# Target one-hots of the edge counts: from one VectorE comparison to two ScalarE activations

## The chip, the cores and the metric

One core of a Trainium2 chip runs the kernel as one program. The time is the device time of one execution in microseconds (us); the median of several runs is given. The core's engines are TensorE (PE in the profile, with its weight loads as PEld), VectorE (DVE), ScalarE (ACT), GpSimd (POOL) and SyncE (SP), which issues most transfers.

## What is computed (the reference)

A graph of N = 1250 nodes with 768 features and 20000 edges (sorted by target) passes two graph networks, each followed by a residual sum and a layer norm:

```python
loops = jnp.arange(N)
src = jnp.concatenate([edge_index[0], loops])
dst = jnp.concatenate([edge_index[1], loops])
x1 = jax.nn.relu(x @ W_ah + b_ah)
# three attention layers on x1, their outputs joined and projected
e = jax.nn.leaky_relu(as_n[src] + ad_n[dst], 0.2)
p = jnp.exp(e - jax.ops.segment_max(e, dst)[dst])
out = segment_sum(p / segment_sum(p, dst)[dst] * h[src], dst)
```

The kernel never walks over edges in the attention layers. It turns the edge list once into a dense table of counts, how many edges lead from node s to node d with the node's own loop added, and multiplies by it. The first stage makes this table, and x1 beside it.

## The kernel before

The first stage is `counts_and_x1`. It works in ten tiles of T = 125 target nodes. The edges stand in 40 columns of 4 x 125; since they are sorted by target, the edges of one tile lie in a few neighbouring columns. DVE works out for every tile the first column, the number of columns and the number of columns before it (lines 216 to 241, into `range_i`). A column is a run of RUN = 4 groups of 125 edges, one edge to a partition.

For a tile, `count(t)` on TensorE first writes the own loops into `p_count` (line 382, three matmuls of a shifted band), and then for every group of 125 edges multiplies two one-hot matrices (line 388): `dst_hot`, 125 edges by 125 target nodes of the tile, is the stationary side, and `src_hot`, 125 edges by 1250 source nodes, the moving side, in three pieces of 418, 416 and 416 columns. Their product adds each edge to the cell of its pair. DVE makes both one-hots by comparing the row of node numbers `node_no` with the edge's own number, a column of `edge_col` (lines 254 and 255), in `one_hots(t)`. Four buffers of each stand in a ring: `hot_ready` tells TensorE that a pair is there, `hot_free` tells DVE that a buffer is read. The number of runs is known only on the chip, so `one_hots` and `count` are loops over a register, and each begins by loading two or three registers from `range_i` (lines 246 to 248 on DVE, 378 and 379 on TensorE).

Around this, in an order written out by hand for each engine, stands other work, five times for a pair of tiles b:

- TensorE: count the even tile, turn a piece of x (line 417), make a part of x1 (line 431, three matmuls for each product of split operands), turn the counted row (line 401), count the odd tile, the rest of x1, turn the next x, turn the odd row, turn x again.
- DVE: one-hots of the even tile, the low parts of x (line 269), score weights (line 502), the mask (line 260), the low part of x1 (line 276), one-hots of the odd tile, then score weights, mask and low parts again.
- ACT: `round_x` (line 322, the rounded part of x), `stage_row` (line 309, the counts from PSUM to SBUF), `keep_x1` (lines 335 and 339), `keep_turned` (line 316, the turned row into the table `CT`). It does nothing while TensorE counts.

ACT's order in the loop is:

```python
round_x(b, 2)
stage_row(b * 2)
keep_x1(b, 0)
keep_turned(b * 2)
stage_row(b * 2 + 1)
keep_x1(b, 1)
keep_x1(b, 2)
round_x(b + 1, 0)
keep_turned(b * 2 + 1)
round_x(b + 1, 1)
```

POOL makes the constants and splits the weights of x1, and SP loads x. At the end of the stage all engines meet at a barrier, after which `project` begins at its line 575 (loads) and line 717 (TensorE).

Of the kernel before, what the change touches and what calls it, by code (L numbers as in the profile page):

```python
# [4 lines left out]
F32 = mybir.dt.float32  # L5
F32R = mybir.dt.float32r
BF16 = mybir.dt.bfloat16
# [3 lines left out]
ALU = mybir.AluOpType  # L11
ACT = mybir.ActivationFunctionType
# [5 lines left out]
T = 125  # L18
NT = N // T
KD = D // 128  # L20
RUN = 4
ER = E // (RUN * T)
# [79 lines left out]
def counts_and_x1(nc, core, src, dst, x, w_ah, b_ah, w_gat, a_gat):  # L102
# [4 lines left out]
    with ExitStack() as ctx:  # L107
        sb, pb, sem = core.tools(ctx)
        dst_ends = sb("dst_ends", [ER, 2], F32)
        ends_row = sb("ends_row", [128, 2, ER], F32)  # L110
        edge_col = sb("edge_col", [T, 2, RUN, 2 * ER], F32)
# [7 lines left out]
        range_i = sb("range_i", [1, 3, NT], I32)  # L119
        node_no = sb("node_no", [T, N], I16)  # L120
        src_hot = sb("src_hot", [T, RUN, N], BF16)
        dst_hot = sb("dst_hot", [T, RUN, T], BF16)
        band = sb("band", [T, 2 * N - T], BF16)
        ident_b = sb("ident_b", [T, T], BF16)
        zeros_b = sb("zeros_b", [T, T], BF16)
# [7 lines left out]
        bias = sb("bias_ah", [128, KD], F32)  # L133
# [16 lines left out]
        cols_ready = sem("cols_ready")  # L150
        ranges_ready = sem("ranges_ready")
        hot_ready = sem("hot_ready")
        hot_free = sem("hot_free")
        counted = sem("counted")
        row_staged = sem("row_staged")
        mask_done = sem("mask_done")
# [32 lines left out]
        @block.gpsimd  # L189
        def _(pool):  # L190
            pool.iota(node_no[:], [[1, N]], base=0, channel_multiplier=0).then_inc(consts, 1)
            pool.iota(tile_lo, [[T, NT], [0, ER]], base=0, channel_multiplier=0).then_inc(consts, 1)
            pool.iota(run_no, [[0, NT], [1, ER]], base=0, channel_multiplier=0).then_inc(consts, 1)
            for m in (band, ident_b, zeros_b):
                pool.memset(m[:], 0.0).then_inc(consts, 1)
            pool.wait_ge(consts, 6)
            pool.affine_select(out=ident_b[:], in_=ident_b[:], compare_op=ALU.not_equal, fill=1.0, base=0,
                               pattern=[[-1, T]], channel_multiplier=1).then_inc(consts, 1)

            pool.affine_select(out=band[:], in_=band[:], compare_op=ALU.not_equal, fill=1.0, base=N - T,  # L200
                               pattern=[[-1, 2 * N - T]], channel_multiplier=1).then_inc(consts, 1)
            for k in range(KD):
                pool.wait_ge(w_in[k % 2], 16 * (k // 2 + 1))
                pool.tensor_copy(w_hi[:, k, :], w_raw[:, k % 2, :]).then_inc(w_split, 1)
                pool.wait_ge(w_split, 2 * k + 1)
                pool.tensor_tensor(w_lo[:, k, :], w_raw[:, k % 2, :], w_hi[:, k, :].bitcast(F32),
                                   ALU.subtract).then_inc(w_split, 1)
            weighed.loads(pool, lambda n: w_gat[n // KD, n % KD * 128:(n % KD + 1) * 128, :].rearrange("p (u c) -> p u c", u=1),
                          lambda g: a_gat[g:g + 1].rearrange("o a c -> o (a c)").broadcast_to([128, 2 * PAIR]))

        @block.vector
        def _(dve):
# [32 lines left out]
            def one_hots(t):  # L245
                first = dve.value_load(range_i[0:1, 0, bass.ds(t, 1)], min_val=0, max_val=ER - 1)
                count = dve.value_load(range_i[0:1, 1, bass.ds(t, 1)], min_val=1, max_val=ER)
                before = dve.value_load(range_i[0:1, 2, bass.ds(t, 1)], min_val=0, max_val=ER * NT)
                with dve.Fori(0, count) as j:
                    for h in range(RUN):  # L250

                        dve.wait_ge(hot_free, (before + j) * RUN + (h + 1))
                        at = bass.ds(first + j, 1)
                        v.tensor_scalar(src_hot[:, h, :], node_no[:], edge_col[:, 0, h, at], None, ALU.is_equal)
                        v.tensor_scalar(dst_hot[:, h, :], node_no[:, bass.ds(t * T, T)], edge_col[:, 1, h, at],  # L255
                                        None, ALU.is_equal).then_inc(hot_ready, 1)

            def mask(t):
                dve.wait_ge(row_staged, t + 1)
# [36 lines left out]
        @block.scalar  # L296
        def _(act):

            nc.scalar.sem_inc(mask_done, 1)

            act.wait_ge(bias_in, 16)

            def stage_row(t):

                act.wait_ge(counted, t + 1)
                act.wait_ge(mask_done, t + 1)
                act.wait_ge(row_turned, t * 3 + 1)
                for i, (a, w) in enumerate(CH):
                    last = nc.scalar.activation(count_row[:, a:a + w], p_count[:, i, 0:w], ACT.Copy)
                last.then_inc(row_staged, 1)  # L310

            def keep_turned(t):
                for i in range(3):
                    k = 4 if i < 2 else 2
                    act.wait_ge(row_turned, t * 3 + (i + 2))
                    nc.scalar.activation(CT[:, 4 * i:4 * i + k, bass.ds(t * T, T)],
                                         p_turn[0:T, i, 0:k * T].rearrange("p (k q) -> p k q", q=T),
                                         ACT.Copy).then_inc(ct_done, 1)

            def round_x(b, g):  # L320
                act.wait_ge(x_turned, b * 3 + (g + 1))
                nc.scalar.activation(xT_hi[:, 2 * g:2 * g + 2, :],
                                     p_x[:, g % 2, 0:2 * BT].rearrange("p (k n) -> p k n", k=2),
                                     ACT.Copy).then_inc(xhi_done, 1)

            def keep_x1(b, g):
                act.wait_ge(x1_summed, b * 3 + (g + 1))
                if g == 0 and b:
                    act.wait_ge(x1_lo_done, b * 3)
                if g == 2:  # L330
                    act.wait_ge(x1_lo_done, b * 3 + 1)
                if g == 1 and b:
                    act.wait_ge(x1_lo_done, b * 3 - 1)
                for m in range(2):
                    last = nc.scalar.activation(x1_f[:, g % 2, m * BT:(m + 1) * BT], p_x[:, (g + 1) % 2, m * BT:(m + 1) * BT],
                                                ACT.Relu, bias=bias[:, 2 * g + m:2 * g + m + 1])
                last.then_inc(x1_relu, 1)
                act.wait_ge(x1_relu, b * 3 + (g + 1))
                nc.scalar.activation(x1T[0][:, 2 * g:2 * g + 2, bass.ds(b * BT, BT)],
                                     x1_f[:, g % 2, :].rearrange("p (k n) -> p k n", k=2),  # L340
                                     ACT.Copy).then_inc(x1_hi_done, 1)

            round_x(0, 0)
            round_x(0, 1)
            for b in range(NB):
                round_x(b, 2)
                stage_row(b * 2)
                keep_x1(b, 0)
                keep_turned(b * 2)
                stage_row(b * 2 + 1)  # L350
                keep_x1(b, 1)
                keep_x1(b, 2)
                if b + 1 < NB:
                    round_x(b + 1, 0)
                keep_turned(b * 2 + 1)
                if b + 1 < NB:
                    round_x(b + 1, 1)

        @block.tensor
        def _(pe):  # L360
# [16 lines left out]
            def count(t):  # L377
                count_ = pe.value_load(range_i[0:1, 1, bass.ds(t, 1)], min_val=1, max_val=ER)
                before = pe.value_load(range_i[0:1, 2, bass.ds(t, 1)], min_val=0, max_val=ER * NT)

                for i, (a, w) in enumerate(CH):
                    nc.tensor.matmul(p_count[:, i, 0:w], ident_b[:], band[:, bass.ds(t * -T + (N - T + a), w)],
                                     start=True, stop=False, skip_group_check=True)
                with pe.Fori(0, count_) as j:
                    for h in range(RUN):
                        pe.wait_ge(hot_ready, (before + j) * RUN + (h + 1))
                        for i, (a, w) in enumerate(CH):
                            last = nc.tensor.matmul(p_count[:, i, 0:w], dst_hot[:, h, :], src_hot[:, h, a:a + w],  # L388
                                                    start=False, stop=False, skip_group_check=True)
                        last.then_inc(hot_free, 1)  # L390
                nc.tensor.matmul(p_count[:, 0, 0:2], zeros_b[:], src_hot[:, 0, 0:2], start=False, stop=True,
                                 skip_group_check=True).then_inc(counted, 1)
# [1633 lines left out]
```

## Time and profile before

| | us |
|---|---|
| median of 3 runs | 2172.72 (2171.94 to 2173.78) |
| the profiled execution, its own time | 2165.81 |
| its span, first to last instruction | 2164.0 |
| mean granted TensorE clock | 0.941 of full speed |
| PE busy | 1872.8 (87%) |
| PEld busy | 1785.0 (82%) |
| DVE busy | 1483.7 (69%) |
| ACT busy | 963.4 (45%) |
| POOL busy | 199.6 (9%) |

All times in the profile count from the span's start. The counting with its x1 work takes the stretch from 26 us to 262 us. An instruction group has a count, a busy time, a mean duration, and the idle time that its engine had just before such instructions, with what ended it ("issue" is time in which the engine waited for nothing that the profile shows). An engine's instructions overlap a little: the next starts before the last has ended, so that a pitch (start to start) is shorter than a duration. A line with a small q behind the engine (DVEq) is the engine's sequencer: registers, branches, waits.

### The profile page before, as it was taken

What the parts mean: (1) busy time and instruction counts of PE and PEld (TensorE: products, weight loads), DVE (VectorE), ACT (ScalarE), POOL (GpSimd) and SP (SyncE); (2) the same over time, 40 slices, a digit from 0 to 9 for tenths busy, and PEclk for the clock granted to TensorE, in tenths of its full rate; (3) what the DMA queues carried; (4) which work ended last, traced back from release to release, by engine and by line L of the source; (5) the groups of instructions that cost most, each with busy time, mean ns of one, the idle gap of its engine ahead of it and who ended that gap; (6) DMA issues with size and microseconds to landing.
All of it is one profiled execution on the core that took longest, in us unless ns stands there. A gap on an engine that the chain in (4) does not pass through costs nothing. (4 is left out here: it accounts for less than half of the span.)

```text
span 2164.0 us, 30233 instructions
## 1 busy us (share of the span) xinstructions
PE 1872.8 (87%) x11452; PEld 1785.0 (82%) x11452; DVE 1483.7 (69%) x2447; ACT 963.4 (45%) x1446; POOL 199.6 (9%) x161
## 2 busy tenths in 40 slices
PE   5999899967999999952999799969999968995993
PEld 4666699967999999952999599969999968995993
DVE  7887689978888889721565449348888863335842
ACT  1222221217779787830232322257888853333411
POOL 5010021200000000000000101100000000004500
PEclk9999999988999999976999899989999989998997
DMA  3121145344234333146655456473243217455002
GB/s 112 47 70 48 63 129 152 98 114 123 80 87 114 105 108 86 60 135 173 191 152 162 128 151 173 134 181 99 84 139 96 75 56 222 108 136 131 1 1 72
DMA packets 203526, 237.73 MB, mean 110 GB/s; under 512 B 99598, under 2 KB 178534, under 8 KB 203394
## 3 DMA queue, kind: packets, MB, share of 16 engines
q1 hardware_dynamic: 193314, 204.09, 33.5%
q0 software_dynamic: 9312, 29.14, 4.7%
q10 hardware_dynamic: 768, 2.70, 0.4%
q8 instruction: 87, 1.43, 0.3%
q14 instruction: 45, 0.37, 0.1%
HBM read 173.99 MB, written 61.90 MB: 109 GB/s over the span
## 5 line engine op out<-in xcount | busy, mean ns | idle before, releaser
L946 PE MATMUL p_o<-h_in,p 125*125 125x193 f32 x2400 | 405.7, 332 | 42.6 <-ACT res L843 21.7
L946 PEld LDWEIGHTS p_o<-h_in,p 125*125 125x125 f32 x2400 | 399.5, 191 | 45.9 <-issue 24.7
L1669 PE MATMUL p_y<-fw_hi,f_hi 128*125 128x384 f32 (+1 forms) x680 | 236.1, 347 | 88.3 <-DVE f_lo L1543 87.5
L866 ACT ACTIVATE e<-uv,col 125x1250 f32<-125x1250 f32 x240 | 298.5, 1359 | 17.3 <-DMA uv<-uv_rows 15.0
L1404 PE MATMUL p_o<-p_hi,h_parts 125*128 125x416 f32 (+1 forms) x960 | 282.6, 355 | 25.2 <-DVE p_lo L1338 19.0
L1669 PE MATMUL p_y<-fw_lo,f_hi 128*125 128x384 f32 (+1 forms) x680 | 233.7, 344 | 0.0
L1669 PE MATMUL p_y<-fw_hi,f_lo 128*125 128x384 f32 (+1 forms) x680 | 233.2, 343 | 0.0
L900 DVE TENSOR_TENSOR e<-e 125x1250 f32<-125x1250 f32 x120 | 174.1, 1451 | 67.6 <-ACT e L866 67.5
L1543 DVE TENSOR_TENSOR f_lo<-f_raw,f_hi 128x1125 fp32r<-128x1125 f32 (+1 forms) x80 | 101.1, 1265 | 169.4 <-ACT f_hi L1643 169.4
L1643 ACT ACTIVATE f_hi<-f_raw 128x1125 fp32r<-128x1125 f32 (+1 forms) x80 | 87.4, 1093 | 275.0 <-PE p_y L1669 221.0
L1404 PEld LDWEIGHTS p_o<-p_hi,h_parts 125*128 125x128 f32 x960 | 181.6, 189 | 31.2 <-issue 19.2
L1669 PEld LDWEIGHTS p_y<-fw_hi,f_hi 128*125 128x125 f32 x680 | 129.7, 191 | 91.4 <-issue 90.0
L646 DVE CUSTOM_DVE_ANT_0 max_junk<-src_row,G 125x1250 bf16<-125x1250 f32 x120 | 185.8, 1615 | 4.3 <-DMA src_row<-score_rows 3.7
L733 PE MATMUL p_h<-pw_hi,x1T 128*125 128x384 f32 x720 | 186.3, 340 | 0.0
L905 DVE SCALAR_TENSOR_TENSOR p<-e,CT 125x1250 f32<-125x1250 f32 x120 | 175.3, 1461 | 6.9 <-PE p_o L946 3.0
L1146 PE MATMUL p_h<-pw_hi,x2T 128*125 128x256 f32 x960 | 172.6, 283 | 0.0
L1404 PE MATMUL p_o<-p_lo,h_parts 125*128 125x416 f32 (+1 forms) x480 | 169.9, 354 | 0.0
L1146 PEld LDWEIGHTS p_h<-pw_hi,x2T 128*125 128x125 f32 x960 | 147.6, 188 | 0.0
L388 PE MATMUL p_count<-src_hot,dst_hot 125*125 125x416 bf16 (+1 forms) x588 | 126.3, 371 | 17.6 <-DVE dst_hot L255 17.6
L1296 ACT ACTIVATE e<-uv,col 125x416 f32<-125x416 f32 (+1 forms) x240 | 139.6, 629 | 0.0
L1146 PE MATMUL p_h<-pw_lo,x2T 128*125 128x256 f32 x480 | 135.8, 283 | 0.0
L388 PEld LDWEIGHTS p_count<-src_hot,dst_hot 125*125 125x125 bf16 x588 | 73.8, 145 | 70.4 <-DVE dst_hot L255 53.8
(220 smaller groups left out, 3330.7 us busy)
## 6 DMA issues: line engine op xcount, KB each, us to landing
f_raw<-turned SPq DMA_DIRECT2D x40, 562.5 KB
f_raw<-turned SPq DMA_DIRECT2D x40, 500.0 KB
h_rows<-h_out SPq DMA_DIRECT2D x32, 560.0 KB
h_parts<-h_rows SPq DMA_DIRECT2D x40, 448.0 KB
uv<-uv_rows SPq DMA_DIRECT2D x24, 546.9 KB
turned<-out_f SPq DMA_DIRECT2D x18, 625.0 KB
h_rows<-h_out SPq DMA_DIRECT2D x24, 424.4 KB
h_in<-h_rows SPq DMA_DIRECT2D x24, 424.4 KB
```

The costliest lines, as they stand in the source:

```text
L388: last = nc.tensor.matmul(p_count[:, i, 0:w], dst_hot[:, h, :], src_hot[:, h, a:a + w], start=False, stop=False, skip_group_check=True)
L646: v.tensor_tensor_reduce(out=junk[:, t % 2, :], in0=src_row[:, h % 2, :], in1=G[:, t, :], scale=1.0, scalar=NO_EDGE, op0=ALU.add, op1=ALU.max,
L733: last = nc.tensor.matmul(p_h[:, (u * NT + t) % 4, 0:width], xp[:, k, at], wp[:, u, k, :], start=(k == 0 and n == 0), stop=(k == KD - 1 an ...
L866: last = a.activation(e[:, g % RING, kind, :], uv[:, hh, kind, :], ACT.Exp, bias=col_src[kind][:, bass.ds(i * 2 + hh, 1), s])
L900: v.tensor_tensor(e[:, g % RING, 0, :], e[:, g % RING, 0, :], e[:, g % RING, 1, :], ALU.max).then_inc(more_ready, 1)
L905: v.scalar_tensor_tensor(p[:, g % RING, :], e[:, g % RING, 0, :], 1.0, CT[:, s, :], ALU.min, ALU.mult).then_inc(p_ready, 1)
L946: last = nc.tensor.matmul(p_o[:, b, n * 256:n * 256 + C0 + 1], p[:, g % RING, d * T:(d + 1) * T], h_in[:, hh, s, 0:C0 + 1], start=(s == 0 ...
L1146: last = nc.tensor.matmul(p_h[:, n % 4, 0:HALF1], xp[:, k, at], wp[:, q % 2, k, :], start=(k == 0 and j == 0), stop=(k == KD - 1 and j == 2))
L1296: last = a.activation(e[:, g % RING, kind, 0:w], uv[:, i % 2, kind, at:at + w], ACT.Exp, bias=col_src[kind][:, i, s:s + 1])
L1404: last = nc.tensor.matmul(p_o[:, bank(n, c), 0:w], h[:, s, kind, cols].bitcast(F32R), pp[:, g % RING, 0:w], start=(s == 0 and j == 0), sto ...
L1543: v.tensor_tensor(f_lo[:, kh], f_raw[:, kh], f_hi[:, kh].bitcast(F32), ALU.subtract).then_inc(f_lo_done, 1)
L1669: last = nc.tensor.matmul(p_y[:, t % 2, 0:CW + extra], fp[:, kh, kk, :], wp[:, k, :], start=(k == 0 and n == 0), stop=(k == K - 1 and n == 2))
```

## The change

The target one-hot is made on ACT, in two activations: the square of (edge's target number - node number), then relu(1 - that square), which is 1 where the two agree and 0 elsewhere. DVE keeps the source one-hot alone and tells `hot_ready` behind it. A run's four squares go first, then its four relus. TensorE waits for both one-hots. ACT calls `dst_hots` ahead of `round_x(b, 2)` for the even tile, and between `keep_turned(b * 2)` and `stage_row(b * 2 + 1)` for the odd one.

```diff
+        apart = sb("dst_apart", [T, RUN, T], BF16)
+        one_col = sb("one_col", [T, 1], F32)
...
+            pool.memset(one_col[:], 1.0).then_inc(one_set, 1)
...
                         at = bass.ds(first + j, 1)
-                        v.tensor_scalar(src_hot[:, h, :], node_no[:], edge_col[:, 0, h, at], None, ALU.is_equal)
-                        v.tensor_scalar(dst_hot[:, h, :], node_no[:, bass.ds(t * T, T)], edge_col[:, 1, h, at],
-                                        None, ALU.is_equal).then_inc(hot_ready, 1)
+                        v.tensor_scalar(src_hot[:, h, :], node_no[:], edge_col[:, 0, h, at], None, ALU.is_equal).then_inc(hot_ready, 1)
...
+            nc.scalar.sem_inc(dst_ready, RUN)
+            act.wait_ge(one_set, 1)
+            act.wait_ge(cols_ready, 1)
+            act.wait_ge(ranges_ready, 1)
+
+            def dst_hots(t):
+
+                first = act.value_load(range_i[0:1, 0, bass.ds(t, 1)], min_val=0, max_val=ER - 1)
+                count = act.value_load(range_i[0:1, 1, bass.ds(t, 1)], min_val=1, max_val=ER)
+                before = act.value_load(range_i[0:1, 2, bass.ds(t, 1)], min_val=0, max_val=ER * NT)
+                with act.Fori(0, count) as j:
+                    at = bass.ds(first + j, 1)
+                    for h in range(RUN):
+                        act.wait_ge(dst_ready, (before + j) * RUN + (h + 1))
+                        nc.scalar.activation(apart[:, h, :], node_no[:, bass.ds(t * T, T)], ACT.Square,
+                                             bias=edge_col[:, 1, h, at], scale=-1.0).then_inc(dst_apart, 1)
+                    for h in range(RUN):
+                        act.wait_ge(dst_apart, (before + j) * RUN + (h + 1))
+                        act.wait_ge(hot_free, (before + j) * RUN + (h + 1))
+                        nc.scalar.activation(dst_hot[:, h, :], apart[:, h, :], ACT.Relu, bias=one_col[:], scale=-1.0).then_inc(dst_ready, 1)
...
             for b in range(NB):
+                dst_hots(b * 2)
                 round_x(b, 2)
                 stage_row(b * 2)
                 keep_x1(b, 0)
                 keep_turned(b * 2)
+                dst_hots(b * 2 + 1)
                 stage_row(b * 2 + 1)
...
                         pe.wait_ge(hot_ready, (before + j) * RUN + (h + 1))
+                        pe.wait_ge(dst_ready, (before + j) * RUN + (h + 1 + RUN))
```

## Rows read from the trace of the kernel before

**Rows 1.** The page's slices: busy tenths in 40 equal slices of the span.
```profile
DVE  7887689978888889721565449348888863335842
ACT  1222221217779787830232322257888853333411
```

**Rows 2.** Groups of 26 to 262 us by shape: count, busy us, mean ns, idle before.
```profile
L254 DVE TENSOR_SCALAR src_hot<-node_no,edge_col 125x1250 bf16<-125x1250 int16 x196 | 106.1, 541 | 14.7 <-issue 12.1 <-PE p_count L388 2.1
...
L388 PEld LDWEIGHTS p_count<-src_hot,dst_hot 125*125 125x125 bf16 x588 | 73.8, 145 | 70.4 <-DVE dst_hot L255 53.8
...
L255 DVE TENSOR_SCALAR dst_hot<-node_no,edge_col 125x125 bf16<-125x125 int16 x196 | 48.6, 248 | 0.0
```

**Rows 3.** Order of time, DVE, start of tile 3: start, us, what, idle before.
```profile
93.81 0.68 DVE L276 TENSOR_TENSOR x1T<-x_f,x1T 128x500 fp32r<-128x500 f32 x1 [0.60 <-ACT x1T L339]
96.02 0.55 DVE L254 TENSOR_SCALAR src_hot<-node_no,edge_col 125x1250 bf16<-125x1250 int16 x1 [1.53 <-issue]
96.48 0.25 DVE L255 TENSOR_SCALAR dst_hot<-node_no,edge_col 125x125 bf16<-125x125 int16 x1
96.65 0.54 DVE L254 TENSOR_SCALAR src_hot<-node_no,edge_col 125x1250 bf16<-125x1250 int16 x1
```

**Rows 4.** Order of time, PEld, a stretch in which it had hot pairs waiting.
```profile
79.06 3.52 PEld L388 LDWEIGHTS p_count<-src_hot,dst_hot 125*125 125x125 bf16 x20
```

**Rows 5.** Window of tile 2's count: PE, PEld, DVE, ACT, POOL busy, granted clock, DMA.
```profile
74.10:87.30 13.20, 13.15 (x62) 8.63 (x63) 12.59 (x39) 0.00 (x0) 0.00 (x0) 0.87 0.00 1
```

**Rows 6.** Order of time, PE, starts of the counts of tiles 2 and 3.
```profile
74.15 13.17 PE L388 MATMUL p_count<-src_hot,dst_hot 125*125 125x418 bf16 x60 [2.00 <-DVE dst_hot L255]
...
96.79 12.46 PE L388 MATMUL p_count<-src_hot,dst_hot 125*125 125x418 bf16 x60 [0.81 <-DVE dst_hot L255]
```

**Rows 7.** Waits of 26 to 262 us: total us, times, longest.
```profile
PE p_count L388 <- DVE dst_hot L255: 17.6, 10, 3.5
```

**Rows 8.** ACT's biased activations: order of time, then their groups.
```profile
1484.41 1.16 ACT L1296 ACTIVATE e<-uv,col 125x416 f32<-125x416 f32 x2
...
697.79 6.27 ACT L866 ACTIVATE e<-uv,col 125x1250 f32<-125x1250 f32 x5
...
92.30 0.83 ACT L335 ACTIVATE x_f<-p_x,bias_ah 128x250 f32<-128x250 f32 x2 [2.63 <-PE p_x L431]
...
L335 ACT ACTIVATE x_f<-p_x,bias_ah 128x250 f32<-128x250 f32 x30 | 12.4, 466 | 30.9 <-PE p_x L431 30.9
...
L1296 ACT ACTIVATE e<-uv,col 125x416 f32<-125x416 f32 (+1 forms) x240 | 139.6, 629 | 0.0
...
L866 ACT ACTIVATE e<-uv,col 125x1250 f32<-125x1250 f32 x240 | 298.5, 1359 | 17.3 <-DMA uv<-uv_rows 15.0
```

**Rows 9.** Order of time, DVE, start of tile 2.
```profile
71.30 0.67 DVE L269 TENSOR_TENSOR xT_lo<-p_x,xT_hi 128x500 fp32r<-128x500 f32 x1
73.38 0.55 DVE L254 TENSOR_SCALAR src_hot<-node_no,edge_col 125x1250 bf16<-125x1250 int16 x1 [1.41 <-issue]
```

**Rows 10.** Order of time, ACT, last work before tiles 2 and 3; group of its third copies.
```profile
72.23 0.61 ACT L322 ACTIVATE xT_hi<-p_x 128x500 fp32r<-128x500 f32 x1
...
94.83 1.34 ACT L316 ACTIVATE CT<-p_turn 125x500 uint16<-125x500 f32 x3 [1.05 <-PE p_turn L401]
...
L316 ACT ACTIVATE CT<-p_turn 125x250 uint16<-125x250 f32 x10 | 3.9, 388 | 0.0
```

**Rows 11.** DVE's sequencer in the loop over runs: ns min/median/max, first and last start.
```profile
L249 DVEq FUSED_REGOPS  x49: 70/70/77, 28.5 to 246.4; - x49
...
L249 DVEq COMPARE_BRANCH  x49: 50/56/69, 30.1 to 248.7; - x49
```

**Rows 12.** ACT's table loads in the whole trace, and the first in order of time.
```profile
L1749 ACT ACT_TABLE_LOAD x2 | 2.6, 1283 | 47.6 <-PEq L62 47.6
...
L1296 ACT ACT_TABLE_LOAD x1 | 1.3, 1283 | 3.1 <-DMA uv<-uv_rows 3.1
...
24.23 1.28 ACT L322 ACT_TABLE_LOAD   x1 [24.23 <-PE p_x L417]
```

More of the change, by code:

```diff
@@ L153, in counts_and_x1 @@
         hot_free = sem("hot_free")
+        one_set = sem("one_set")
+        dst_apart = sem("dst_apart")
+        dst_ready = sem("dst_ready")
         counted = sem("counted")
```

## Prediction

> **What bounds the kernel now.** I read the slices of the page first: PE is busy 87% of the whole span, and of the first five slices DVE takes seven or eight tenths, ACT one or two [rows 1]. The change touches only the first 12% of the span, so the question is what sets the pace there. The groups of that stretch [rows 2] show 196 source one-hots of 0.541 us and 196 target one-hots of 0.248 us on DVE, and TensorE weight loads that stand idle 70.4 us, 53.8 of it for the target one-hot. The order of time within one counting stretch [rows 3] gives the pace: a source one-hot at 96.02, its target one-hot 0.46 us later, the next source one-hot 0.17 after that. A stretch of 60 matmuls in which TensorE always waited for DVE (the one at 96.79 [rows 6]) took 12.46 us; less the last three, 0.53 and their tail of 0.17, that is 19 pairs, 0.619 each. I use 0.618 and 0.16. PE's own pace shows where it had work waiting [rows 4]: 20 weight loads in 3.52 us, the last 0.14 long, is (3.52 - 0.14)/19 = 0.178 us each, three to a hot pair, 0.534 us. So DVE sets the pace at 0.618 and PE could go at 0.534. Tile 2 had the same 60 matmuls at a mean granted clock of 0.87 [rows 5] and took 13.17 us [rows 6]; such a dip stands in four of the ten stretches, and there PE is the slower for a while.
>
> At the start of each tile PE also waits. Before tile 3 it has its band matmuls done and waits 0.81 us for the first hot pair, before tile 2 it waits 2.00 [rows 6]; over the ten tiles it is 17.6 us, 3.5 of it at the first [rows 7].
>
> **Removed.** 196 target one-hots leave DVE. Each costs it 0.618 - 0.46 = 0.16 us of pace, so DVE alone would run at 0.46, below PE. The slower of PE (0.534) and ScalarE then decides.
>
> **Added on ScalarE.** Two activations of 125x125 from and to SBUF, each with a bias column. No row has that size. The nearest in kind are those with a bias column from SBUF [rows 8]: two of 416 columns last 1.16 us together and 0.63 alone, a pitch of 0.534; five of 1250 columns last 6.27 and 1.36 alone, a pitch of 1.23. The slope is 0.69/834 = 0.83 ns per column, so 125 columns give a pitch of 0.534 - 291 x 0.00083 = 0.292 and a duration of 0.39 us. The lower bound comes from the PSUM form of 250 columns: 0.83 for two, 0.466 for one, pitch 0.364, less 125 columns 0.26 us [rows 8]. The upper bound is each pass waiting out the one before it, 0.39 plus some 0.03: 0.42. I take 0.292, from the row nearest in kind: 0.584 us for a pair, 2.34 us for a run of four, against 2.47 now.
>
> **The pace, summed.** There are 49 runs of four (196 hots) in ten tiles. Now: 196 x 0.618, less 0.08 at each tile's end where the last pair takes PE's 0.534, is 120.3 us. After: all squares of a run precede its relus, so PE gets four hots close together and takes 4 x 0.534 = 2.14 us for them. The first 39 runs cost 2.34 each, the last of each tile 2.14: 91.3 + 21.4 = 112.7. Gain **7.6 us**. At PE's own pace it would be 196 x 0.534 = 104.7, a gain of 15.6: that is the cap.
>
> **The start of a tile.** Now DVE loads three registers and makes the first hot pair while ACT still copies the turned row out. After the change ACT does the registers itself, and in its own order only behind those copies (odd tiles) or behind the rounding of x (even tiles). DVE needed 2.21 us from the start of its last instruction at 93.81 to its first one-hot at 96.02 [rows 3], and 2.08 from 71.30 to 73.38 [rows 9]; I take 2.1 for ACT. Then come four squares at 0.292 (1.17), the relu's duration 0.39 and 0.05 until PE starts: 3.7 us from the start of ACT's last older instruction. In tile 3 that is the third copy, of 0.388 us: 94.83 + 1.34 - 0.39 = 95.78 [rows 10], so PE starts at 99.5, not at 96.79 [rows 6]: 2.7 late. In tile 2 it is the rounding at 72.23 [rows 10], so 75.9, not 74.15: 1.8 late. Counted as PE's whole wait, that is 3.5 us in an odd tile (2.7 + 0.81) and 3.8 in an even one (1.8 + 2.00). Nine tiles: 5 x 3.5 + 4 x 3.8 = 32.7, less the 17.6 - 3.5 = 14.1 waited now [rows 7] is 18.6. The first tile starts behind ACT's table load and first roundings [rows 12] as DVE does now; it has the fills, 1.6 us, less DVE's 0.7 for its own first pair: I take 0.6. Cost **19.2 us**. With the pitch's lower bound 0.26 it is about 18, and with ACT queueing 0.3 us ahead of its engine about 16.5.
>
> **What else.** The other order on ACT stands: row staging waits for the count's end anyway. DVE's score weights get 0.16 x 20 = 3 us of slack per tile, worth nothing, since ACT's start is now last. PE has a second wait per hot, hidden as long as ScalarE is slower than 0.534; if PE decides, it costs between nothing and one register operation of 0.05 to 0.07 us, as DVE's [rows 11], at 196 hots up to 14 us. I take nothing. The extra memset of one column on POOL stands ahead of weight splits that PE needs only behind the first count; nothing. Two functions are asked of ScalarE in turn, and Square is new to the kernel. The rows have table loads at lines 322, 1296 and 1749 alone [rows 12]: copies, relus and the exponentials of line 866 all run on the first, so this set is wide, and I cost the switch at nothing. A load takes 1.283 us, the first one in an engine that had been idle for 24.23 [rows 12]. The Trainium skill, "ScalarE: Activation LUTs", What ACT_TABLE_LOAD costs, counts a drain of 1.38 us ahead of each switch as well; here ACT had nothing to drain, so the trace can't show it. With Square in the set both add nothing; what each would make of it otherwise is rival (c).
>
> Behind the stage all engines meet at the barrier, so what the stage loses shifts the rest whole. The squares are 0, 1 and more, and bf16 keeps these apart, so the counts stay.
>
> Sum: -7.6 + 19.2 = +11.6 us. The profiled execution took 2165.8 with a span of 2164.0; the three timed runs have the median 2172.7, 6.9 above, and the sum is added to that: **2184 us**. About 0.2%, 4.3 us, is what a measurement of this kernel can tell from no change.
>
> **Rivals.**
> (a) Not slower: PE becomes the bound. If the pitch is at the PSUM row's 0.26, a pair takes 0.52, under PE's 0.534. The gain is then the cap, 15.6; the start costs 16.5 to 18: +1 to +2.5 us, 2174. It ends clearly below the old time only where half of ACT's 2.1 us of register loads also runs under its copies, 1 us less in each of nine tiles: 2166. The point from which it decides is a pair at 0.55 us. For it: ACT is idle in all counting stretches. Against it: the SBUF forms are both above.
> (b) The loop's turn shows. DVE's loop has a branch and register work between runs (0.07 and 0.06 us for two of them, plus the gaps around [rows 11]), hidden there by 0.54 us one-hots. ACT's relus wait for two semaphores each and can't be issued far ahead; if 0.4 us per run stays in the open, 39 runs cost 15.6 more: +27, 2200. Even the full serial bound of 0.42 per pass (3.36 a run) gives +51, 2224; I hold that unlikely.
> (c) A table reload. If Square isn't in the set that is loaded [rows 12], each run of four switches twice: 98 x 1.283 = 126 us more, 2310. With the drain that the Trainium skill's page counts, an estimate from its figure, it would be 98 x 2.66 = 261 us. Against it stands how many kinds run on one load, for it that no row shows Square.
>
> **How the numbers follow.** Forecast (ScalarE's pace, late starts, +5 to +19) 0.53; (a) 0.19, of which 0.06 ends more than 4.3 us below the old time and 0.13 within it; (b) 0.23; (c) 0.05. The range reaches down to 2171, most of (a), and up to 2204, most of (b). Slower: 0.53 + 0.23 + 0.05 = 0.81.
>
> **What would show it.** Right: 392 new ScalarE activations of 0.36 to 0.42 us; the source one-hots wait for PE matmuls; a tile's matmul stretch of 60 near 11.6 us, not 12.4; PE's wait for the first relu near 3.5 us on nine tiles; the stage's last mask and turned row some 11.6 us later than now. Wrong: a stretch of 60 near 10.9 (rival a) or above 13 (rival b), more than the few table loads (rival c), or waits at the tile's start that are no longer than now.

## The result, and the profile after

| | before | after |
|---|---|---|
| median us, 8 runs each | 2171.12 (2168.34 to 2173.78) | 2182.65 (2178.88 to 2188.30) |
| ratio | | 1.0054, 95% interval 1.0040 to 1.0069 |
| span of the profiled execution | 2164.0 | 2177.8 |

The change costs 11.5 us, half a per cent. The slices of the page answer to [rows 1]: ACT has gone from one or two tenths to six or seven in the counting slices.

```profile
DVE  6777659996888888832565539447888863345842
ACT  3777622216787879731232322247888863323321
```

The groups of 0 to 290 us by shape answer to [rows 2] (count, busy us, mean ns, idle before and what ended it):

```profile
L416 PEld LDWEIGHTS p_count<-src_hot,dst_hot 125*125 125x125 bf16 x588 | 84.7, 150 | 70.9 <-ACT dst_hot L326 43.5
L260 DVE TENSOR_SCALAR src_hot<-node_no,edge_col 125x1250 bf16<-125x1250 int16 x196 | 102.9, 548 | 37.8 <-PE p_count L416 25.1 <-issue 12.5
L326 ACT ACTIVATE dst_hot<-dst_apart,one_col 125x125 bf16<-125x125 bf16 x196 | 64.0, 387 | 9.2 <-PE p_count L416 8.6
L321 ACT ACTIVATE dst_apart<-node_no,edge_col 125x125 bf16<-125x125 int16 x196 | 61.7, 387 | 8.0 <-issue 7.6
```

Both activations last 0.387 us, and VectorE now waits for TensorE's matmuls (25.1 us, against 2.1 before): it has left the bound. The order of time on ACT around tile 3 answers to [rows 10] and goes on into the new work:

```profile
95.07 1.34 ACT L341 ACTIVATE CT<-p_turn 125x500 uint16<-125x500 f32 x3 [1.05 <-PE p_turn L429]
97.61 1.27 ACT L321 ACTIVATE dst_apart<-node_no,edge_col 125x125 bf16<-125x125 int16 x4 [1.20 <-issue]
98.78 1.25 ACT L326 ACTIVATE dst_hot<-dst_apart,one_col 125x125 bf16<-125x125 bf16 x4
99.94 1.25 ACT L321 ACTIVATE dst_apart<-node_no,edge_col 125x125 bf16<-125x125 int16 x4
```

Four squares begin at 97.61 and four relus at 98.78, the next squares at 99.94: a pitch of 0.29 us, a run of four in 2.33. And ahead of tile 2, where the rounding of x is ACT's last older work:

```profile
73.53 0.61 ACT L347 ACTIVATE xT_hi<-p_x 128x500 fp32r<-128x500 f32 x1
74.32 1.27 ACT L321 ACTIVATE dst_apart<-node_no,edge_col 125x125 bf16<-125x125 int16 x4 [0.18 <-issue]
```

PE's order of time for tiles 1, 2 and 3 answers to [rows 6], and the waits of 26 to 274 us to [rows 7]:

```profile
52.32 11.71 PE L416 MATMUL p_count<-src_hot,dst_hot 125*125 125x418 bf16 x60 [3.32 <-ACT dst_hot L326]
...
75.93 11.62 PE L416 MATMUL p_count<-src_hot,dst_hot 125*125 125x418 bf16 x60 [2.52 <-ACT dst_hot L326]
...
99.22 14.13 PE L416 MATMUL p_count<-src_hot,dst_hot 125*125 125x418 bf16 x60 [3.00 <-ACT dst_hot L326]
```

```profile
PE p_count L416 <- ACT dst_hot L326: 25.4, 9, 3.3
...
PE p_count L416 <- DVE src_hot L260: 3.4, 1, 3.4
```

PE's waits at the tiles' starts are 25.4 + 3.4 = 28.8 us where they were 17.6. The stretches of 60 matmuls differ: 11.71, 11.62, and then 14.13. The windows of tiles 1 and 3, and of the first 3.5 us of tile 3 alone (busy of PE, PEld, DVE, ACT, POOL, then the granted clock), say why:

```profile
52.30:64.10 11.80, 11.75 (x63) 8.14 (x63) 10.28 (x29) 10.20 (x35) 0.32 (x1) 1.00 0.00 0
99.20:113.40 14.20, 14.16 (x62) 9.86 (x63) 10.31 (x29) 10.88 (x35) 0.26 (x1) 0.79 0.00 0
...
99.20:102.70 3.50, 3.48 (x10) 2.34 (x11) 1.10 (x2) 2.68 (x9) 0.00 (x0) 0.50 0.00 0
```

At the start of tile 3's count TensorE had the lower of its two clock levels (0.50 of full speed), and it fell behind. A count that ran partly at the lower level is said to have a fall from here on. Of the nine counts behind the first, six have one here, four had before. The first count begins slowly in both kernels; these are two windows of it in the kernel before:

```profile
29.50:33.00 3.50, 3.48 (x10) 2.35 (x11) 3.16 (x10) 0.00 (x0) 0.00 (x0) 1.00 0.26 105
...
36.50:40.00 3.50, 3.50 (x21) 2.40 (x19) 3.50 (x13) 0.00 (x0) 0.00 (x0) 1.00 0.00 0
```

The first row prints a clock of 1.00 only because this trace's first clock record is at 34.5 us: it has 10 matmuls in 3.5 us, as the row at 0.50 above, and the second has 21. It is so in all ten profiles without a fill (a term of the experiments below), and four of them, that of the changed kernel among them, recorded it. The expectations below count such a recorded one as a fall and say seven of ten for the changed kernel; text and tables count tiles 1 to 9. The same two rows for each of the ten tiles give the account of the stage, with its end read from POOL's first memset of the next one:

| us | before | after |
|---|---|---|
| PE's waits at the ten starts | 17.6 | 28.8 |
| the ten stretches of count matmuls | 126.3 | 126.5 |
| falls in tiles 1 to 9 | 4 | 6 |
| a stretch of 60 matmuls without one | 12.45 | 11.6 to 11.7 |
| end of the stage | 260.9 | 272.4 |
| rest of the span | 1903.1 | 1905.4 |

So 11.2 of the 11.5 us that the stage lost are waits at the starts, and the faster pace, plain to see in an undisturbed stretch, has gained nothing in the sum of the stretches. The two profiled spans differ by 13.8 us; the 2.3 behind the stage are within what code that is the same in all kernels shows from one profile to the next (1902.3 to 1911.6 us).

### The profile page after: what moved, and what is told of

It reads as the page before. It is cut to its first block and busy times, and to the rows that moved or that the text cites. A ratio compares the mean times of both kernels' runs of the same rounds, so it can differ in the third digit from the quotient of the medians.

```text
span 2177.8 us, 31218 instructions
## 1 busy us (share of the span) xinstructions
PE 1870.5 (86%) x11452; PEld 1792.7 (82%) x11452; DVE 1464.4 (67%) x2251; ACT 1081.8 (50%) x1838; POOL 199.2 (9%) x162
## 5 line engine op out<-in xcount | busy, mean ns | idle before, releaser
L894 ACT ACTIVATE e<-uv,col 125x1250 f32<-125x1250 f32 x240 | 298.5, 1359 | 17.1 <-DMA uv<-uv_rows 15.0
L674 DVE CUSTOM_DVE_ANT_0 max_junk<-src_row,G 125x1250 bf16<-125x1250 f32 x120 | 180.9, 1581 | 9.4 <-DMA src_row<-score_rows 8.8
L416 PE MATMUL p_count<-src_hot,dst_hot 125*125 125x416 bf16 (+1 forms) x588 | 126.3, 373 | 28.9 <-ACT dst_hot L326 25.4
L416 PEld LDWEIGHTS p_count<-src_hot,dst_hot 125*125 125x125 bf16 x588 | 84.7, 150 | 70.9 <-ACT dst_hot L326 43.5
```

What stands on the lines that cost most here:

```text
L674: v.tensor_tensor_reduce(out=junk[:, t % 2, :], in0=src_row[:, h % 2, :], in1=G[:, t, :], scale=1.0, scalar=NO_EDGE, op0=ALU.add, op1=ALU.max,
L894: last = a.activation(e[:, g % RING, kind, :], uv[:, hh, kind, :], ACT.Exp, bias=col_src[kind][:, bass.ds(i * 2 + hh, 1), s])
```

## The experiments

Theory A was the prediction's: two costs in a sum, later starts and ScalarE's pace. Theory B, in the expectations, puts the loss down to the clock. Two things were open: whether the starts alone carry the loss, and why the pace brought nothing. All kernels are timed against the kernel before on the same chip, the experiments in three rounds on three chips, so ratios compare better than medians. "Waits" are PE's at the ten starts, "stretches" the sum of the ten.

**The pace.** The squares go; ScalarE makes one relu of (target - node), so this kernel counts something else.

```diff
-  four times Square into apart, then four times Relu(1 - apart) into dst_hot
+  four times Relu(target - node) into dst_hot
```

> The squares are left out: ScalarE makes one relu per group straight from the node numbers, so dst_hot isn't a one-hot and the counts differ. Theory A (two costs in a sum: TensorE waits longer at a tile's start, and the pace of a counting stretch is ScalarE's 0.58 us per pair): the pace becomes TensorE's 0.534, a stretch of 60 matmuls at full clock 10.9 us instead of 11.65; four squares of 0.29 leave the start of each tile until the source one-hot is the last, so PE's start waits fall from 28.8 to about 19 us in sum; together 2165 us, 17 below the changed kernel. Theory B (a faster stretch only brings more dips of the granted clock, which eat it): the waits fall alike, but the ten stretches still sum to about 126 us and the time is near 2173.

Ratio 0.9977 (0.9965 to 0.9989), median 2165.99. Waits 21.2, stretches 115.8, four falls. The window of tile 3's count:

```profile
95.00:105.90 10.90, 10.90 (x62) 8.40 (x63) 10.10 (x28) 7.20 (x19) 0.07 (x1) 1.00 0.00 0
```

60 matmuls in 10.90 us at full clock: TensorE is the bound at once when ScalarE's pair shrinks, so it was ScalarE's pace that gave 11.6. Theory B falls as it was put: a still faster pace had fewer falls (four) than the changed kernel (six), not more.

**The starts.** The older copies and the rounding move behind the one-hots.

```diff
                 dst_hots(b * 2)
+                if b:
+                    keep_turned(b * 2 - 1)
+                    round_x(b, 1)
                 round_x(b, 2)
...
-                keep_turned(b * 2)
                 dst_hots(b * 2 + 1)
+                keep_turned(b * 2)
...
-                keep_turned(b * 2 + 1)
-                if b + 1 < NB:
-                    round_x(b + 1, 1)
+            keep_turned(NT - 1)
```

> ScalarE makes a tile's target one-hots ahead of the copies of the turned row and the rounding that it did first; all else as changed. Theory A: PE's start waits fall from 28.8 to about 14 us, some 0.5 us per even tile come back behind the count where the rounding is now late, and the time is near 2169, at or under the kernel before. Theory B (the loss is not in the starts but in the granted clock): PE rests less, dips get no rarer, and the time stays near 2182.

Ratio 0.9953 (0.9936 to 0.9970), median 2161.76: 21 us under the changed kernel, where 14 were expected. Waits 16.4, stretches 117.4, two falls. PE's start of tile 3 and the windows of tiles 2 and 3:

```profile
95.65 1.63 PE L417 MATMUL p_count<-src_hot,dst_hot 125*125 125x418 bf16 x8 [0.75 <-ACT dst_hot L326]
```

```profile
72.90:85.90 13.00, 12.98 (x63) 9.16 (x64) 9.67 (x19) 11.69 (x37) 0.00 (x0) 0.87 0.00 1
95.60:107.30 11.70, 11.65 (x63) 8.15 (x64) 11.21 (x32) 11.30 (x39) 0.28 (x1) 1.00 0.00 0
```

Of the stage's 19.7 us (its end is at 252.7), 12.4 are waits, and 9.0 are shorter stretches, with work of 1.7 us come back in between. The shorter stretches were in no sum: their pace is nearly the same, the falls are gone in the odd tiles, which PE now enters after a wait of 0.7 to 1.7 us, and have stayed in two of the even ones, after waits of 1.94 and 1.96. The rival's "no change" falls.

**The order inside a run.**

```diff
-  square 0, 1, 2, 3, then relu 0, 1, 2, 3
+  square 0, square 1, relu 0, square 2, relu 1, square 3, relu 2, relu 3
```

> Only the order inside a run of four changes: square 0, square 1, relu 0, square 2, relu 1 and so on. Theory A: the first relu comes two squares (0.58 us) earlier in each of nine tiles, start waits 23.6 instead of 28.8 us, the pace as before the edit (11.65 for 60 matmuls at full clock), time near 2177. Rival: relus now wait for squares that have only just ended and the pair costs 0.7 us, so that the stretch grows to 14 us and the time to over 2200.

Ratio 1.0018 (1.0008 to 1.0028), median 2174.42. ACT at tile 3:

```profile
99.76 0.69 ACT L321 ACTIVATE dst_apart<-node_no,edge_col 125x125 bf16<-125x125 int16 x2 [1.20 <-issue]
100.36 0.39 ACT L330 ACTIVATE dst_hot<-dst_apart,one_col 125x125 bf16<-125x125 bf16 x1
100.65 0.39 ACT L321 ACTIVATE dst_apart<-node_no,edge_col 125x125 bf16<-125x125 int16 x1
```

The waits are 23.6 as expected, the pitch stays at 0.29 and an undisturbed stretch at 11.71. A relu that needs a square of one place earlier loses nothing. But eight stretches had a fall, and they sum to 125.4.

**The late start alone.** Added to the kernel before, where VectorE still makes both one-hots:

```diff
+                if b:
+                    dve.wait_ge(xhi_done, b * 3 + 2)
                 one_hots(b * 2)
...
+                dve.wait_ge(ct_done, (b * 2 + 1) * 3 + 1)
                 one_hots(b * 2 + 1)
```

> The kernel before, with one thing added: VectorE waits, ahead of each tile's one-hots, for the ScalarE work (the third copy of the turned row, or the rounding of x) that stands ahead of the target one-hots in the changed kernel. Theory A: the late start alone costs its wait: PE's start waits go from 17.6 to about 34 us and the time from 2171 to 2187. Theory B (TensorE's rest is paid back by fewer dips of the granted clock): less than half of it shows, 2179 or less.

Ratio 1.0108 (1.0085 to 1.0131), median 2194.52. One of its four executions took 4308.37 us, twice the rest, for a reason that stays unknown; it stands in this median but not in the ratio, and the other three have the median 2192.44. Neither theory holds, for it is worse than both. Waits 34.7, as Theory A had it (+17.1). But the stretches went up too, from 126.3 to 130.3, and all nine counts behind the first had a fall. Tiles 2 and 1:

```profile
78.00:92.10 14.10, 14.02 (x62) 9.32 (x63) 12.83 (x40) 0.00 (x0) 0.00 (x0) 0.80 0.00 1
51.90:65.00 13.10, 13.10 (x62) 8.61 (x63) 12.67 (x45) 0.00 (x0) 0.00 (x0) 0.87 0.00 0
```

Here the pace is the old one and ScalarE has no part in it. What four kernels had in common was then put as Theory R: the clock falls at the start of a count because PE has rested before it. It was tested by filling the rest.

**Filling PE's wait** in the changed kernel:

```diff
+                for i in range(12):
+                    nc.tensor.matmul(p_count[:, 2, 0:416], zeros_b[:], band[:, 0:416], start=False, stop=False,
+                                     skip_group_check=True)
                 with pe.Fori(0, count_) as j:
```

> The changed kernel with 12 matmuls of zeros behind the three band matmuls of each tile, 12 x 0.178 = 2.1 us of work that adds nothing to the counts, inside PE's wait for the first relu (2.5 to 3.3 us). Theory R (the granted clock falls at the start of a count because PE has rested before it): falls in at most three of ten counting stretches instead of seven, the stretches sum to 116 to 119 us instead of 126.5, the starts as late as before, time near 2174. Rival (the falls come by chance, or with the faster pace): stretches near 126, time near 2182.

Ratio 0.9998 (0.9986 to 1.0009), median 2171.47: 11 us less for doing more. PE before tile 3 and the window of its count:

```profile
94.43 0.69 PE L409 MATMUL p_count<-band,ident_b 125*125 125x418 bf16 x3
94.96 2.27 PE L412 MATMUL p_count<-band,zeros_b 125*125 125x416 bf16 x12
98.13 1.10 PE L419 MATMUL p_count<-src_hot,dst_hot 125*125 125x418 bf16 x5 [0.89 <-ACT dst_hot L326]
```

```profile
98.10:109.80 11.70, 11.67 (x62) 8.13 (x63) 10.23 (x29) 10.12 (x35) 0.26 (x1) 1.00 0.00 0
```

The first hot matmul still comes 3.0 us behind the end of the band matmuls (0.89 waited and 2.1 filled). There is no fall in any of the ten stretches, the first count runs at full pace from its start (9.17 us, 10.84 without the fill), and they sum to 113.8. Theory R holds: with the pace and the starts as they were, the fill alone took the falls away. The stretches are now 12.5 us under those of the kernel before, which pays for the 11.2 of late starts, and the kernel stands level with it. Not all of the 12.5 is the pace, since the kernel before has falls of its own. Whether the wait alone brings a fall, or the wait together with the small matmuls ahead of it, no run here separates.

**Register loads early** in the changed kernel: ScalarE loads the next tile's three registers behind `dst_hots` of this one.

```diff
+            regs = registers(0)
             for b in range(NB):
-                dst_hots(b * 2)
+                dst_hots(b * 2, *regs)
+                regs = registers(b * 2 + 1)
                 round_x(b, 2)
```

> The changed kernel, but ScalarE loads the three registers of the next tile behind the loop of the one before, not ahead of its own. Theory A (register loads of 1.6 us are half of the start cost): the squares start some 1.25 us earlier; odd tiles' waits fall from 3.0 to 1.75, even ones' from 2.5 to about 1.75 where the source one-hot is then last; in sum from 28.8 to about 19.5 us, time near 2173, and near 2166 if the falls of the clock become as rare as in the kernel before. Rival: the loads already run under older work and nothing moves.

Ratio 0.9992 (0.9979 to 1.0004), median 2169.87. Waits 21.2, stretches 118.1, two falls. Nothing stands between the copies and the squares any more:

```profile
94.53 1.34 ACT L344 ACTIVATE CT<-p_turn 125x500 uint16<-125x500 f32 x3 [1.05 <-PE p_turn L436]
95.74 1.27 ACT L324 ACTIVATE dst_apart<-node_no,edge_col 125x125 bf16<-125x125 int16 x4
```

Odd tiles wait 1.7 to 2.0 instead of 3.0, about as expected; even ones only fell from 2.5 to 2.2, since their loads had mostly run under the copies before (0.18 idle at 74.32 above), so the sum is 1.7 us above what was expected.

**Both together, on both engines**: e2's order, and the loads of the next tile behind `stage_row` or `keep_x1` on ACT and behind `rest_of_x` or `rest_of_x1` on DVE. The edit is shown against e2.

```diff
-                one_hots(b * 2)
+                one_hots(b * 2, *regs)
                 rest_of_x(b, 1)
+                regs = registers(b * 2 + 1)
...
                 stage_row(b * 2)
+                regs = registers(b * 2 + 1)
                 keep_x1(b, 0)
-                dst_hots(b * 2 + 1)
+                dst_hots(b * 2 + 1, *regs)
                 keep_turned(b * 2)
```

> Hots first as in e2, and the register loads early on ScalarE and VectorE, where both wait for other things. Theory A and R: PE's start waits fall from 16.4 (e2) to about 6 us, the counting stretches stay near 116, no rest of 2 us before a count is left and so few falls of the clock; time near 2150. If the loads only move the wait to the work behind them, it stays near 2162.

Ratio 0.9910 (0.9885 to 0.9935), median 2153.07. Waits 7.8, stretches 117.2, one fall, at the one tile (5) that PE entered after 2.05 us, where VectorE was late. In tile 3 PE goes from the band straight into the count:

```profile
90.87 0.69 PE L424 MATMUL p_count<-band,ident_b 125*125 125x418 bf16 x3
91.40 11.44 PE L431 MATMUL p_count<-src_hot,dst_hot 125*125 125x418 bf16 x60
```

**The fill on e2**, with 8 matmuls:

> e2 with 8 matmuls of zeros (1.4 us) behind the band matmuls. In even tiles they lie inside PE's wait of 1.95 us, in odd ones they overrun its 0.75 by 0.7 us. Theory R: no fall of the clock at the even tiles (three in e2, 1.4 us each), while odd tiles lose 5 x 0.7: time 2161 to 2163, stretches summing to 113 instead of 117. Rival: falls as in e2, time 2165.

Ratio 0.9918 (0.9899 to 0.9936), median 2156.50, 5 us under e2 where little was expected. No fall; the stretches sum to 112.6 as expected. Odd tiles lost less than the 0.7 each that I had set down: from the end of the band matmuls to the first hot one they took 1.24 us, at most 0.5 more than in e2.

**The fill on the late start** (e4 with 14 matmuls of zeros):

> e4 (the kernel before with late starts) with 14 matmuls of zeros, 2.5 us, inside PE's waits of 3.2 and 3.7 us. Theory R: e4's 23 us over the kernel before are 17 us of later starts and the rest falls of the granted clock (nine of ten stretches); with the fill the stretches are back at 12.45 us for 60 matmuls, no fall in them, and the time is near 2189, still 17 above the kernel before. Rival (the fill itself shortens the start): the time falls below 2185.

Ratio 1.0054 (1.0037 to 1.0071), median 2184.85: 12 above the kernel before, not 17. No fall, each stretch of 60 at 12.45 to 12.49, the ten at 122.1:

```profile
51.20:63.70 12.50, 12.45 (x62) 6.85 (x63) 12.50 (x45) 0.00 (x0) 0.00 (x0) 1.00 0.00 0
```

The expectation was off because it forgot that the kernel before has four falls and a slow first count of its own, which the fill takes away as well: the stretches are 4.2 under its 126.3, so 16 to 17 us of later starts leave 12 to 13, and the stage ends at 273.9, 13.0 later than before. The median lies on the border of the rival, that the fill shortens the start. PE's rows at tile 3 decide against it:

```profile
97.25 0.69 PE L385 MATMUL p_count<-band,ident_b 125*125 125x418 bf16 x3
97.78 2.62 PE L388 MATMUL p_count<-band,zeros_b 125*125 125x416 bf16 x14
101.14 2.24 PE L394 MATMUL p_count<-src_hot,dst_hot 125*125 125x418 bf16 x10 [0.74 <-DVE dst_hot L255]
```

The first hot matmul comes 3.20 us behind the end of the band matmuls, exactly as in e4. So e4's stage, which ended 21.1 us later than before, lost 17.1 in waits and 4.0 in stretches; the fill takes 8.2 us off its stretches, more than those 4.0, since the kernel before has its own 4.2.

**The fill on the kernel before**, 9 matmuls in even tiles alone:

> The kernel before with 9 matmuls of zeros, 1.6 us, in the five even tiles, where PE waits 2.0 us and all four of its falls of the clock stand. Theory R: no fall in the ten stretches, each worth 0.65 us there since VectorE's pace hides the rest: 2 to 3 us, time 2169. If the fall's cost is hidden wholly: 2171.

Ratio 0.9972 (0.9961 to 0.9982), median 2165.28. Of the four falls none is left in an even tile; the expectation had all four there, but one stood in tile 7, and this time tile 7 was entered after 1.13 us and had none, while one stands in tile 5, which has no fill and had a wait of 1.99 in this execution. The stretches sum to 123.0, 3.3 less, and the stage ends 3.3 earlier; 1.3 of it is the first count, now at full pace from its start (10.01 us for 11.27). The timed gain is 3.9 to 8.5 us, more than the stage shows. The profiled execution of the kernel before was a quick one, 2165.81 us where the median beside this run is 2172.62, so its falls may have been fewer than usual; whether that is the rest stays open.

**TensorE as the bound**: e7, with VectorE comparing every fourth target as before.

```diff
+                        if h == RUN - 1:
+                            last = v.tensor_scalar(dst_hot[:, h, :], node_no[:, bass.ds(t * T, T)], edge_col[:, 1, h, at],
+                                                   None, ALU.is_equal)
...
-                    for h in range(RUN):
+                    for h in range(RUN - 1):
```

> e7 (hots first, registers early), but the target one-hot of every fourth group is VectorE's comparison as in the kernel before: ScalarE has 6 activations of 0.29 = 1.74 us for a run of four, VectorE 4 x 0.46 + 0.16 = 2.0, TensorE 2.14. If the pace is the slowest engine's, TensorE is now the bound: 60 matmuls at full clock in 10.9 instead of 11.6 us, 7 us in all, time near 2146. If the mixed order costs a wait, the stretches stay at 11.6 and the time at 2153.

Ratio 0.9884 (0.9868 to 0.9901), median 2146.17, the fastest version: 25 us, 1.2%, under the kernel before.

```profile
87.11 0.69 PE L428 MATMUL p_count<-band,ident_b 125*125 125x418 bf16 x3
87.64 10.85 PE L436 MATMUL p_count<-src_hot,dst_hot 125*125 125x418 bf16 x60
```

```profile
87.60:98.50 10.90, 10.90 (x64) 8.36 (x62) 10.71 (x32) 8.93 (x27) 0.00 (x0) 1.00 0.04 14
```

The pace is TensorE's 0.534, and the waits (7.8) are as in e7. There is no fall in tiles 1 to 9, though tile 5 was entered after 2.16 us.

**The changed kernel again:**

> The changed kernel once more, unchanged. Theory R: falls of the granted clock again in six or more of ten counting stretches, stretches summing to 123 to 128 us, PE's start waits 28.8 us as in its first profile. If the falls are chance: any number, the sum down to 114.

Ratio 1.0069 (1.0052 to 1.0086), median 2186.06. Waits 28.8 again to a tenth; eight falls, and stretches of 131.6, beyond the 128 that was the upper end. Tiles 2 and 3:

```profile
79.30:92.50 13.20, 13.13 (x62) 9.06 (x63) 9.91 (x19) 10.58 (x35) 0.00 (x0) 0.87 0.01 1
104.10:118.40 14.30, 14.22 (x62) 9.87 (x63) 10.27 (x29) 10.95 (x36) 0.22 (x1) 0.79 0.00 0
```

So which tiles get a fall, and whether a long or a short one, varies from one execution to the next (tile 2 had none in the first profile). That doesn't explain the spread of the times: this kernel's eight spread over 9 us, but so do the 19 of the kernel before beside e5 (2166.37 to 2176.01), and the ten of e5, whose profile has no fall, over 8.

All fourteen profiles side by side, with the falls in tiles 1 to 9:

| kernel | waits | stretches | falls | ratio |
|---|---|---|---|---|
| before | 17.6 | 126.3 | 4 | 1 |
| after | 28.8 | 126.5 | 6 | 1.0054 |
| e12 after again | 28.8 | 131.6 | 8 | 1.0069 |
| e5 after, filled | 7.3 + fill | 113.8 | 0 | 0.9998 |
| e4 before, late | 34.7 | 130.3 | 9 | 1.0108 |
| e9 before, late, filled | 9.1 + fill | 122.1 | 0 | 1.0054 |
| e10 before, filled | 9.6 + fill | 123.0 | 1 | 0.9972 |
| e3 order in a run | 23.6 | 125.4 | 8 | 1.0018 |
| e1 relus only | 21.2 | 115.8 | 4 | 0.9977 |
| e6 registers early | 21.2 | 118.1 | 2 | 0.9992 |
| e2 hots first | 16.4 | 117.4 | 2 | 0.9953 |
| e8 hots first, filled | 2.9 + fill | 112.6 | 0 | 0.9918 |
| e7 both early | 7.8 | 117.2 | 1 | 0.9910 |
| e11 three to one | 7.8 | 108.5 | 0 | 0.9884 |

## Why the prediction was right, and where it was not

The direction, the time (2184 for 2182.65) and the range held. The mechanism held in part: ScalarE's own order makes each tile start late, and this costs more than its pace gives, but by 2.9 us (11.2 against 8.3) and not by 11.6. The rest of the loss is the slower clock, which the prediction took for unchanged. Point by point:

- *ScalarE's pitch of 0.292 and duration of 0.39, from the SBUF forms [rows 8]*: 0.29 and 0.387. The lower bound from the PSUM form would have been wrong by a tenth.
- *A stretch of 60 near 11.6*: 11.62 and 11.71, with no fall of the clock. *PE's own 0.534 as the cap*: shown by e1 and e11, 10.9. In e1 PE still waits for two semaphores at each pair, so the second wait cost nothing, as taken.
- *Gain of 7.6 us*: compare the kernels without any fall: 122.1 in e9 (old pace) and 113.8 in e5 (new pace), 8.3 us. Right in size. The working's 120.3 and 112.7 leave out the last matmul's tail of 0.17 in ten tiles; with it they are 122.0 and 114.4.
- *Start cost of 19.2 us*: this term was mis-sized; it measured 11.2 (28.8 against 17.6). The four squares, the relu and PE's start behind it took 99.22 - 97.61 = 1.61 us, exactly the 1.61 of the working. The 2.1 us from the start of ACT's last older instruction to its first square was wrong: 97.61 less the third copy's start, 95.07 + 1.34 - 0.39 = 96.02, is 1.59 in an odd tile, and 74.32 - 73.53 = 0.79 in an even one. ACT's sequencer loads registers while older activations are still queued: in the odd tile its first load began at 95.73, ahead of the third copy at 96.02, and in the even one only 0.18 us of idle time was left at 74.32. The prediction gave 0.3 us for that as a side case and left it out of the sum. The first tile, put at 0.6, cost nothing. The sign that was named, waits near 3.5 us on nine tiles, didn't come: they were 3.0 to 3.3 in odd tiles and 2.5 in even ones.
- *Missing altogether*: what a later start does to the clock. The sum took the four falls that it had seen as a fixed part of the kernel, and didn't see the slow first count. Against the filled kernels the lower clock, falls and first count together, costs 126.3 - 122.1 = 4.2 us before and 126.5 - 113.8 = 12.7 after (17.8 in e12), so 8.5 us more in the first profile.

The measured sum is then +11.2 - 8.3 + 8.5 = +11.4 us, against the stage's own 11.5. The predicted one was +19.2 - 7.6 = +11.6. The totals agree because a cost that was not there (8 us of start) stood in for one that was not seen (8.5 us of clock). The time was right partly by luck. The clock's share is also the least certain: each kernel's stage is read from one execution, and with e12's the same sum is +11.2 - 8.3 + 13.6 = +16.5, where e12's median is 13.4 above its kernel before.

Rival (a), TensorE as the bound, didn't come about by itself and needed e11 to be built; it decides from a pair at its own 0.534, and the working's 0.55 has no sum behind it. Rival (b), the loop's turn in the open, was wrong: the relus at 98.78 and the next squares at 99.94 follow at the same pitch. Rival (c) too: the whole trace has the same table loads as [rows 12] and none in the loop, so Square runs on the set that was there. The Trainium skill, "ScalarE: Activation LUTs", What ACT_TABLE_LOAD costs, puts each switch with its drain at 2.66 us, by which the loss would have been an estimated 261 us; no run here has a switch in the loop.

```profile
L1777 ACT ACT_TABLE_LOAD x2 | 2.6, 1283 | 47.6 <-PEq L62 47.6
L347 ACT ACT_TABLE_LOAD x1 | 1.3, 1283 | 24.3 <-PE p_x L445 24.3
L1324 ACT ACT_TABLE_LOAD x1 | 1.3, 1283 | 3.1 <-DMA uv<-uv_rows 3.1
```

## What to carry to other kernels

Work moved to an idle engine brings the time of its new place in that engine's order: here moving the order alone (e2) turned a loss of 0.5% into a gain of 0.5%. Balance the moved work by pace, against the slowest engine: a quarter given back to VectorE (e11) made TensorE the bound. And price a longer wait of TensorE twice, as the wait and as the slower clock that can follow it; a fill of idle matmuls tells the two apart in one run.

## What the hardware showed that was not expected

The granted clock fell where TensorE had waited, late in the wait or at the beginning of the count that followed. Over all fourteen profiles, tiles 1 to 9: where PE's wait for the first hot pair was 1.9 us or longer, 45 of 59 counts ran into the lower level (0.50 of full speed); where it was shorter, none of 67 did. The longest wait without a fall was 3.32 us, and the same tile with the same wait could go either way (tile 1 of the changed kernel had none in its first profile and one in e12). The fill turned six falls into none in the changed kernel and nine into none in the late one, with the count's start as late as before. The matmuls of the fill had zeros as their stationary side. The Trainium skill, "TensorE: Matmul & The Clock Gate", Part 1, says that being slow is the default state and activity releases it. The traces here agree in direction: the first count of the kernel before began with 10 matmuls in 3.5 us and had 21 in 3.5 us near its end.

A fall costs more the nearer PE is to being the bound behind it. With VectorE's pace of 0.618 a stretch of 60 with one short fall lost 0.6 to 0.7 us (12.45 to 13.1 or 13.2). With ScalarE's 0.58 it lost 1.2 to 1.5 in most kernels (11.65 to 12.9 to 13.2), but 0.9 in e3 (11.71 to 12.65), for a reason that stays open. With PE as the bound, in e1, it lost 1.4 to 1.65 (10.9 to 12.33 or 12.55). The likely reason is that less of the lost time can be made up; it was not tested by itself.
